# Second attention: the next group's weight tiles transposed by VectorE in 32x32 blocks instead of by TensorE

## The chip, the cores and the metric

The kernel runs on one core of a Trainium2 chip. The metric is the device time of one execution in microseconds (us), given as the median of several runs. A profiled execution has a time of its own and, inside it, a span: the stretch from the first to the last instruction that the profiler recorded.

## The reference

A transformer block on `x` (8 x 128 x 512, float32). First comes a low-rank stage with a small attention over the eight rows, then the attention that this case is about, then a feed-forward part with low-rank experts. The second attention, cut to what matters:

```python
q = jnp.einsum('bsd,ed->bse', x, Wq).reshape(bsz, seqlen, HQ, D)   # 32 query heads of 128
k = jnp.einsum('bsd,ed->bse', x, Wk).reshape(bsz, seqlen, HK, D)   # 8 key/value heads
v = jnp.einsum('bsd,ed->bse', x, Wv).reshape(bsz, seqlen, HK, D)
q, k = _rope(_rmsnorm(q, q_norm_w), pos), _rope(_rmsnorm(k, k_norm_w), pos)
kc, vc = k_cache[block_table], v_cache[block_table]                # 512 cached keys per row
scores = einsum(q, concat(kc, k)) * SCALE                          # masked where not valid
probs = jax.nn.softmax(scores, axis=-1)
o = jnp.einsum('bhqk,bkhd->bqhd', probs, concat(vc, v))
return jnp.einsum('bse,de->bsd', o.reshape(bsz, seqlen, HQ * D), Wo)
```

## The kernel before

TensorE multiplies in fp32r, a rounded float32. To keep precision every operand X is split into a high part X_hi (X rounded to fp32r) and a low part X_lo = X - X_hi, and every product is three matmuls (`mm3`, lines 739 to 741). So each operand has to be transposed, rounded and subtracted before it is used.

The second attention is a loop over 8 groups g (one key/value head with its 4 query heads) and, inside it, 8 steps n (one row of the batch): 64 steps. A step of the instruction streams holds, for batch row n: the scores of 4 heads (`ps_a`, `ps_b`), the values product of the step before (`ps_o<-pT,v`), the projection of the next row's q (`ps_q`) and k, v (`project_kv`, into `ps_o` from `wa`), and the output projection of the step before (`out_proj`, from `wo`). Everything is written out by hand, engine by engine, and joined by semaphores; each engine works through its own list in order.

Transposes on TensorE go through a ring of two PSUM banks, `ps_t`. A group of four 128x128 transposes (`transposed`, line 948) fills a bank. ScalarE copies it out rounded (`copy_hi`, line 1366), VectorE subtracts (`copy_lo`, line 1788), and the bank after next waits for that subtraction (`t_lo`). Each step has the ring groups K (cached keys), D0 to D3 (the probabilities of the four heads), q, and DS (the probabilities of the step's own keys).

While group g is worked on, the ten weight tiles of group g+1 (four of Wq, one each of Wk and Wv, four of Wo; 128x512 each) are brought in. `W_COUNT` puts one of them into steps n = 0, 2, 4, 6, two into n = 1, 3, 5, and none into n = 7, in groups 0 to 6: 70 tiles in all. The group of step n = 7 already projects with them. A tile is loaded by SyncE into one of two slots of `wtile` (line 486), transposed as a ring group W between the scores of heads 0 and 1 and the values product, copied by ScalarE into `wa_hi` or `wo_hi` and subtracted by VectorE into `wa_lo` or `wo_lo`. SyncE loads the tile after next into the slot when TensorE is through with it.

The other names that the prediction uses, in the order of one step:

- `least(h)` on VectorE (line 1912) reads head h's scores, adds the mask and finds the extreme, `mn`. ScalarE's `exponentials(h)` (line 1443) follows. `normalise(0)` and `normalise(1)` are on VectorE (lines 1919, 1924), `normalise(2)` and `normalise(3)` on ScalarE (line 1453). D0 to D3 transpose the results.
- `output_hi` and `output_lo` (lines 1413, 1867) split the values product. `own_v_hi` (line 1449) rounds the row's own v.
- `copy_kv` (line 1370) takes the projected k and v out of `ps_o`, and TensorE's `out_proj` waits for it (`kv_copied`). `square_k` (line 1376) sums the squares of k.
- GpSimd does, in a step: four gathers of cached keys (line 622), the high and low parts of v (lines 687, 689, 692), three gathers of cached values, `stats_k` (lines 653, 656: the norm of k, which waits for `square_k`), the fourth gather of values, and `stats_q` (lines 661 to 666: the norm of q). VectorE's `rope_k` (line 1821) waits for `stats_k`. TensorE's `project_kv` waits for the own v's low part (`vs_lo`, line 692). `least(0)` of the next step waits for `stats_q` (`st_done`).
- After `rope_k`, VectorE makes `qT_lo`. The last ring group DS waits for it and ends TensorE's step.

Of the kernel before, what the change touches and what calls it, by code (L numbers as in the profile page):

```python
# [17 lines left out]
F32 = mybir.dt.float32  # L18
# [37 lines left out]
def block_program(nc, x, ids_adapter, table_pages, cache_len, lora_a, lora_b, w_qkv, w_proj, wq, wk, wv, wo,  # L56
# [4 lines left out]
    with ctx:  # L61
# [69 lines left out]
        wa_lo = at("wa_lo", [P, 2, NC_, PW], F32R, 160)  # L131
        wtile = at("wtile", [P, 2, HID], F32, 184)
# [133 lines left out]
        wt_in = [sem(f"wt_in{i}") for i in range(2)]  # L266
        tab_in = [sem(f"tab_in{i}") for i in range(2)]
# [72 lines left out]
        def groups_of(n, last):  # L340
            if last:
                w = [f"L{i}" for i in range(7) if i // 2 + 1 == n] + [f"Y{i}" for i in range(2) if N - 2 + i == n]
            else:
                w = [f"W{W_FIRST[n] + i}" for i in range(W_COUNT[n])] if W_COUNT[n] else []
            nxt = not (last and n == N - 1)
            return w + ["K"] * nxt + ["D0", "D1", "D2"] + ["q"] * nxt + ["D3", "DS"]

# [64 lines left out]
        def hi_lo_target(name, g, kpar1, lo):  # L412
# [13 lines left out]
            return w_dst((wa_hi, wa_lo)[lo], (wo_hi, wo_lo)[lo], (g + 1) % 2, int(name[1:])), HID  # L426
# [20 lines left out]
        def _(sp):  # L447
# [28 lines left out]
            def load_wtile(g, t, slot):  # L476
# [9 lines left out]
                sp.dma_start(wtile[:, slot, :], src).then_inc(wt_in[slot], 16)  # L486
# [37 lines left out]
            def step(g, n, last):  # L524
# [6 lines left out]
                for name in groups_of(n, last):  # L531
                    if name[0] == "W" and int(name[1:]) + 2 < TILES_W:
                        t = int(name[1:])
                        wait_alone(sp, t_full, base + t_index(n, name, last)[0] + 1)
                        load_wtile(g + 1, t + 2, t % 2)
                    elif name[0] == "W" and g + 2 < G:
                        t = int(name[1:])
                        wait_alone(sp, t_full, base + t_index(n, name, last)[0] + 1)
# [39 lines left out]
        def _(pool):  # L578
# [92 lines left out]
            def step(g, n, last):  # L671
# [29 lines left out]
                if not (last and n == N - 1):  # L701
                    stats_q(J + 1, 1 - par)
                if n == N - 1 and not last:
# [40 lines left out]
        def _(pe):  # L744
# [206 lines left out]
            def w_tile(idx, bank, t, arrivals):  # L951
                pe.wait_ge(wt_in[t % 2], arrivals)
                transposed(idx, bank, [(c, wtile[:, t % 2, c * P:(c + 1) * P]) for c in range(NC_)])

# [108 lines left out]
            def step(g, n, first, last):  # L1063
# [39 lines left out]
                for name in names:  # L1103
# [6 lines left out]
                    if name[0] == "W":  # L1110
                        t = int(name[1:])
                        w_tile(*idx(name), t, g * (16 * TILES_W // 2) + 16 * (t // 2 + 1))
# [5 lines left out]
                if nxt:  # L1118
# [3 lines left out]
                    if n == N - 1:  # L1122
                        pe.wait_ge(t_lo, base + t_index(6, "W9", last)[0] + 1 + 2)
# [290 lines left out]

# [674 lines left out]
```

## Time and profile before

| | |
|---|---|
| time, median of 3 runs | 1568.53 us (1563.63 to 1569.09) |
| profiled execution | 1554.2 us, span 1552.5 us |
| busy share of the span | TensorE 97%, VectorE 76%, ScalarE 58%, GpSimd 57% |
| mean granted TensorE clock | 0.991 |
| transposes of `wtile` on TensorE | 280 (70 tiles of four) |

The second attention is the stretch from about 332 us to 1500 us of the span. The profiled execution is some 14 us shorter than the median. In each timeline below a row gives start, duration, engine, line, operation, what is written from what is read, and, in brackets, how long the engine was idle before it and what ended that. An engine starts its next instruction a little before the shown end of the one before, so two starts give the real pace.

### The profile page before, as it was taken

The numbers are of one execution on the slowest core, as the hardware profiler recorded it, in microseconds if no ns is written. First come the engines' busy times: TensorE is split into PE (matmuls) and PEld (weight loads), VectorE is DVE, ScalarE is ACT, GpSimd is POOL, SyncE is SP. The second block draws the span as 40 slices with busy tenths as digits, with TensorE's granted clock in tenths as the row PEclk, the third lists the DMA queues.
The fourth block names the chain that finished last, engine by engine and source line by source line (L and its number), as shares of the span: only waits on it lengthen the run. The fifth ranks groups of instructions, "written<-read, shape, count | busy, mean of one in ns | idle before, by whom it ended". The sixth has DMA issues, their size and how long they took to land.

```text
span 1552.5 us, 27376 instructions
## 1 busy us (share of the span) xinstructions
PE 1509.9 (97%) x8984; PEld 1293.2 (83%) x8984; DVE 1180.2 (76%) x2668; ACT 893.2 (58%) x2308; POOL 879.2 (57%) x1231
## 2 busy tenths in 40 slices
PE   6899999989999999999999999999999999999997
PEld 4788888778888888888888888888888888888885
DVE  3666665767888888888888878888887888777865
ACT  2433333356666666666666666666666666666641
POOL 1111234236667666766676676667666766676521
PEclk8999999999999999999999999999999999999999
DMA  6654555322222222222222222222222222311102
GB/s 209 209 161 134 148 165 162 77 82 70 69 71 73 69 71 61 76 70 70 64 72 71 71 66 70 70 71 72 70 72 66 70 69 65 89 59 48 42 27 82
DMA packets 74085, 133.39 MB, mean 86 GB/s; under 512 B 17426, under 2 KB 27026, under 8 KB 73946
## 3 DMA queue, kind: packets, MB, share of 16 engines
q1 hardware_dynamic: 56482, 97.56, 21.2%
q0 software_dynamic: 16464, 33.85, 7.5%
q8 instruction: 74, 1.21, 0.3%
q14 instruction: 65, 0.53, 0.1%
q10 hardware_dynamic: 1000, 0.23, 0.1%
HBM read 107.47 MB, written 7.34 MB: 74 GB/s over the span
## 4 chain that ended last, share of the span: by engine, by line
PE 91%; DVE 3%; ACT 2%; issue 2%; POOL 1%; DMA 1%; ACTq 0%; POOLq 0%; DVEq 0%; SPq 0%
PE ps_t L948 15%; PE ps_o L739 11%; PE ps_o L741 10%; PE ps_o L740 10%; PE ps_b L739 5%; PE ps_b L741 5%; PE ps_b L740 5%; PE ps_q L741 4%; PE ps_q L740 4%; PE ps_q L739 4%; PE ps_t L762 3%; PE ps_a L739 3%; PE ps_a L793 3%; PE ps_a L741 3%; PE ps_a L740 3%
## 5 line engine op out<-in xcount | busy, mean ns | idle before, releaser
L1443 ACT ACTIVATE sm<-sm,mn 128x640 f32<-128x640 f32 x256 | 211.4, 826 | 234.5 <-DVE mn L1912 234.5
L1788 DVE TENSOR_TENSOR pT_lo<-ps_t,pT_hi 128x512 fp32r<-128x512 f32 x320 | 220.2, 688 | 113.5 <-ACT pT_hi L1366 113.3
L622 POOL DMA_INDIRECT kraw<-in_L_cond_k_cache_dram,idx_a x200 | 197.5, 988 | 89.1 <-issue 74.3
L1366 ACT ACTIVATE pT_hi<-ps_t 128x512 fp32r<-128x512 f32 x320 | 188.5, 589 | 84.7 <-PE ps_t L948 84.7
L622 POOL DMA_INDIRECT vraw<-in_L_cond_v_cache_dram,idx_a x200 | 198.7, 994 | 59.6 <-issue 59.3
L948 PE MATMUL ps_t<-ident,sm 128*128 128x128 f32 x1280 | 195.7, 275 | 3.2 <-ACT sm L1453 1.5
L948 PEld LDWEIGHTS ps_t<-ident,sm 128*128 128x128 f32 x1280 | 147.9, 140 | 51.4 <-DVE qT_lo L1788 17.9
L639 POOL TENSOR_TENSOR z<-pairs_p,zl 128x128 f32<-128x128 f32 x160 | 57.9, 402 | 206.8 <-DVE pairs_p L1652 206.8
L739 PE MATMUL ps_o<-pT_lo,v_hi 128*128 128x512 f32 x320 | 129.8, 406 | 0.0
L741 PE MATMUL ps_o<-pT_hi,v_hi 128*128 128x512 f32 x320 | 125.5, 392 | 0.0
L740 PE MATMUL ps_o<-pT_hi,v_lo 128*128 128x512 f32 x320 | 124.9, 390 | 0.0
L1912 DVE CUSTOM_DVE_ANT_0 sm<-ps_a,mask,qs 128x640 f32<-128x640 f32 x128 | 112.6, 879 | 11.2 <-PE ps_a L741 4.6
L739 PE MATMUL ps_o<-wo_lo,oT_hi 128*128 128x512 f32 x256 | 117.6, 460 | 2.3
L1912 DVE CUSTOM_DVE_ANT_0 sm<-ps_b,mask,qs 128x640 f32<-128x640 f32 x128 | 112.9, 882 | 3.8 <-issue 0.4
L739 PE MATMUL ps_q<-wa_lo,x2T_hi 128*128 128x512 f32 x256 | 105.8, 413 | 0.0
L1453 ACT ACTIVATE sm<-sm,rd 128x640 f32<-128x640 f32 x128 | 105.6, 825 | 0.0
L741 PE MATMUL ps_q<-wa_hi,x2T_hi 128*128 128x512 f32 x256 | 101.5, 396 | 0.0
L741 PE MATMUL ps_o<-wo_hi,oT_hi 128*128 128x512 f32 x256 | 101.4, 396 | 0.0
L740 PE MATMUL ps_o<-wo_hi,oT_lo 128*128 128x512 f32 x256 | 100.6, 393 | 0.0
L740 PE MATMUL ps_q<-wa_hi,x2T_lo 128*128 128x512 f32 x256 | 100.6, 393 | 0.0
L739 PE MATMUL ps_a<-kT_lo,qT_hi 128*128 128x320 f32 x256 | 90.3, 353 | 1.7 <-DVEq L1861 1.7
L689 POOL TENSOR_TENSOR v_lo<-vraw,v_hi 128x512 fp32r<-128x512 f32 x64 | 82.6, 1291 | 11.9 <-POOL v_hi L687 11.5
(257 smaller groups left out, 4370.1 us busy)
## 6 DMA issues: line engine op xcount, KB each, us to landing
fv<-st SPq DMA_DIRECT2D x128, 128.0 KB, 2.3
tab<-tab_scratch SPq DMA_DIRECT2D x64, 256.0 KB
wraw<-n_L_attn_weight_qkv_dram SPq DMA_DIRECT2D x8, 1536.0 KB, 7.3
wpraw<-_L_attn_weight_proj_dram SPq DMA_DIRECT2D x8, 1024.0 KB, 9.4
mask<-mask_scratch SPq DMA_DIRECT2D x64, 128.0 KB
wtile<-in_L_cond_Wq_dram SPq DMA_DIRECT2D x28, 256.0 KB
wtile<-in_L_cond_Wo_dram SPq DMA_DIRECT2D x28, 256.0 KB
kraw<-in_L_cond_k_cache_dram,idx_a POOLq DMA_INDIRECT x200, 2.6
```

The source lines that it names most:

```text
L622: pool.indirect_dma_start(raw[:, par, c, :], None, rows_d, bass.IndirectOffsetOnAxis(idx[:, k:k + 1].bitcast(U32), 0)).then_inc(arrived[pa ...
L639: ins = pool.tensor_tensor(out, pr, zz, ALU.mult)
L689: pool.tensor_tensor(v_lo[:, 0:KC, :], vraw[:, par, :, :], v_hi[:, 0:KC, :].bitcast(F32), ALU.subtract).then_inc(vc_lo, 1)
L739: pe.matmul(o, l_hi, r_lo, start=start, stop=False)
L740: pe.matmul(o, l_lo, r_hi, start=False, stop=False)
L741: return pe.matmul(o, l_hi, r_hi, start=False, stop=stop)
L948: mm = pe.transpose(ps_t[bank][:, o * P:(o + 1) * P], i, ident[:])
L1366: act.activation(dst, src, ACT.Copy).then_inc(t_hi, 1)
L1443: act.activation(sm[:, h, :], sm[:, h, :], ACT.Exp, bias=mn[:, h:h + 1], scale=-1.0, accum_out=den[:, h:h + 1]).then_inc(e_done, 1)
L1453: act.activation(sm[:, h, :], sm[:, h, :], ACT.Copy, scale=rd[:, h:h + 1]).then_inc(p_act, 1)
L1788: dve.tensor_tensor(lo, src, hi.bitcast(F32), ALU.subtract).then_inc(t_lo, 1)
L1912: dve.tensor_tensor_reduce(out=sm[:, h, :].rearrange("p (b k) -> p b k", b=2), in0=halves, in1=mask[:, par, :].rearrange("p (b k) -> p b k ...
```

## The change

- SyncE loads a tile in four DMAs, one for each fourth of the partitions, so that piece (c, i) of 32 inputs of every weight row (128 bytes) lands in partitions 32i to 32i+31. Partition 32i+p holds weight rows 4p to 4p+3.
- VectorE turns the whole tile with one instruction that transposes 32x32 blocks (`turn`), into `wa_turn` or `wo_turn`. These lie where `wa_lo` and `wo_lo` lie. Neighbouring elements of a transposed row are written four float32, 16 bytes, apart.
- ScalarE makes the high part from that (`turned_hi`), at the same place of its list as before.
- GpSimd makes the low part in place at the end of its step, after `stats_q` and ahead of the next step's gathers.
- TensorE's ring group W is gone. The steps of group 7 and its late weights keep theirs.

```diff
+        wa_turn = at("wa_turn", [P, 2, NC_, PW], F32, 160)
+        wo_turn = at("wo_turn", [P, 2, HG, HID], F32, 64)
...
-                sp.dma_start(wtile[:, slot, :], src).then_inc(wt_in[slot], 16)
+                blocks = src.rearrange("e (c i a) -> i e c a", c=NC_, i=4)
+                for i in range(4):
+                    sp.dma_start(wtile[32 * i:32 * i + 32, slot, :], blocks[i]).then_inc(wt_in[slot], 16)
...
+                for t in tiles_of(n, last):
+                    wait_alone(pool, wt_hi, g * TILES_W + t + 1)
+                    pool.tensor_tensor(w_dst(wa_lo, wo_lo, (g + 1) % 2, t), w_dst(wa_turn, wo_turn, (g + 1) % 2, t),
+                                       w_dst(wa_hi, wo_hi, (g + 1) % 2, t).bitcast(F32),
+                                       ALU.subtract).then_inc(wt_lo, 1)
...
-                    if name[0] == "W":
-                        t = int(name[1:])
-                        w_tile(*idx(name), t, g * (16 * TILES_W // 2) + 16 * (t // 2 + 1))
...
-                        pe.wait_ge(t_lo, base + t_index(6, "W9", last)[0] + 1 + 2)
+                        pe.wait_ge(wt_lo, (g + 1) * TILES_W)
...
                 exponentials(0)
                 if w:
                     group(w[0])
+                if tiles:
+                    turned_hi(g, tiles[0])
                 exponentials(1)
                 if len(w) > 1:
                     group(w[1])
+                if len(tiles) > 1:
+                    turned_hi(g, tiles[1])
                 if not first:
                     output_hi(J)
...
+                def turn(t):
+
+                    dve.wait_ge(wt_in[t % 2], (g * (TILES_W // 2) + t // 2 + 1) * 64)
+                    dve.transpose(w_dst(wa_turn, wo_turn, (g + 1) % 2, t).rearrange("p c (b j) -> p j c b", j=4),
+                                  wtile[:, t % 2, :].rearrange("p (j c a) -> p j c a", j=4, c=NC_)
+                                  ).then_inc(wt_turned, 1)
...
                 least(1)
                 if w:
                     group(w[0])
+                if tiles:
+                    turn(tiles[0])
                 normalise(0)
                 normalise(1)
                 if len(w) > 1:
                     group(w[1])
+                if len(tiles) > 1:
+                    turn(tiles[1])
                 if not (first and n < 1):
                     output_lo(J)
```

Two places where this moves instructions. The first is VectorE in a step with two tiles, before:

```order
L1788 TENSOR_TENSOR wa_lo<-ps_t,wa_hi 128x4x128 [waits t_hi]
L1919 RECIPROCAL rd<-den 128x1 [waits e_done]
L1924 TENSOR_SCALAR sm<-sm,rd 128x640 [waits r_done]
L1919 RECIPROCAL rd<-den 128x1 [waits e_done]
L1924 TENSOR_SCALAR sm<-sm,rd 128x640 [waits r_done]
L1788 TENSOR_TENSOR wa_lo<-ps_t,wa_hi 128x4x128 [waits t_hi]
L1867 TENSOR_TENSOR oT_lo<-ps_o,oT_hi 128x512 [waits o_hi]
```

The same place after the change, again VectorE's list in a step with two tiles:

```order
L1911 STREAM_TRANSPOSE wa_turn<-wtile 128x4x4x32 [waits wt_in1]
L1944 RECIPROCAL rd<-den 128x1 [waits e_done]
L1949 TENSOR_SCALAR sm<-sm,rd 128x640 [waits r_done]
L1944 RECIPROCAL rd<-den 128x1 [waits e_done]
L1949 TENSOR_SCALAR sm<-sm,rd 128x640 [waits r_done]
L1911 STREAM_TRANSPOSE wa_turn<-wtile 128x4x4x32 [waits wt_in0]
L1884 TENSOR_TENSOR oT_lo<-ps_o,oT_hi 128x512 [waits o_hi]
```

The subtraction of the tile stood behind ScalarE's rounding; now the transpose stands ahead of it, in the same two positions, and waits for the load. Line numbers differ because the changed file is longer.

The second place is GpSimd's list from `stats_q` of a step with two tiles to the own v's low part of the next step, after the change:

```order
L669 TENSOR_SCALAR ms<-ss 128x4 [waits sqq_done]
L672 TENSOR_TENSOR rs<-ms,halfs 128x4 [waits st_pool]
L674 TENSOR_SCALAR qs<-rs 128x4 [waits st_pool]
L713 TENSOR_TENSOR wa_lo<-wa_turn,wa_hi 128x4x128 [waits wt_hi] x2
L630 DMA kraw<-in_L_cond_k_cache_dram,idx_a 128x128 [waits t_full]
L630 DMA kraw<-in_L_cond_k_cache_dram,idx_a 128x128 x3
L695 CAST v_hi<-vraw 128x512 [waits vg_in0,pv_full]
L697 TENSOR_TENSOR v_lo<-vraw,v_hi 128x512 [waits vc_hi]
L700 TENSOR_TENSOR v_lo<-kvown,v_hi 128x128 [waits vs_hi]
```

The row `wa_lo<-wa_turn,wa_hi` is new on this engine; the rows around it stood next to each other before.

## Rows read from the trace of the kernel before

**Rows 1.** TensorE's timeline: starts of five steps (L739 `ps_a`), three places between

```profile
805.72 0.39 PE L739 MATMUL ps_a<-kT_lo,qT_hi 128*128 128x320 f32 x1
...
817.29 0.28 PE L739 MATMUL ps_o<-wa_lo,x2T_hi 128*128 128x256 f32 x1
...
823.74 0.39 PE L739 MATMUL ps_a<-kT_lo,qT_hi 128*128 128x320 f32 x1
...
837.18 0.60 PE L948 MATMUL ps_t<-ident,sm 128*128 128x128 f32 x4
837.82 0.50 PE L739 MATMUL ps_o<-wo_lo,oT_hi 128*128 128x512 f32 x1
...
842.18 0.39 PE L739 MATMUL ps_a<-kT_lo,qT_hi 128*128 128x320 f32 x1
...
896.67 0.39 PE L739 MATMUL ps_a<-kT_lo,qT_hi 128*128 128x320 f32 x1
...
914.24 0.39 PE L739 MATMUL ps_a<-kT_lo,qT_hi 128*128 128x320 f32 x1
```

**Rows 2.** GpSimd's timeline: one cycle in full places, then the change of group

```profile
820.61 0.19 POOL L653 TENSOR_SCALAR ms<-ss 128x1 f32<-128x1 f32 x1 [1.80 <-ACT rope_b L1376]
...
824.83 0.23 POOL L666 TENSOR_SCALAR qs<-rs 128x4 f32<-128x4 f32 x1 [0.20 <-POOL rs L664]
...
831.24 1.29 POOL L689 TENSOR_TENSOR v_lo<-vraw,v_hi 128x512 fp32r<-128x512 f32 x1 [0.19 <-POOL v_hi L687]
832.49 0.46 POOL L692 TENSOR_TENSOR v_lo<-kvown,v_hi 128x128 fp32r<-128x128 f32 x1
...
839.06 0.19 POOL L653 TENSOR_SCALAR ms<-ss 128x1 f32<-128x1 f32 x1 [2.25 <-ACT rope_b L1376]
...
911.11 0.19 POOL L653 TENSOR_SCALAR ms<-ss 128x1 f32<-128x1 f32 x1 [1.06 <-ACT rope_b L1376]
...
929.15 0.19 POOL L653 TENSOR_SCALAR ms<-ss 128x1 f32<-128x1 f32 x1
```

**Rows 3.** VectorE's timeline: `rope_k` of one step, then a step with two tiles

```profile
821.59 0.35 DVE L1821 SCALAR_TENSOR_TENSOR rope_a<-kvown,rs,tab 128x128 f32<-128x128 f32 x1
...
826.52 0.88 DVE L1912 CUSTOM_DVE_ANT_0 sm<-ps_b,mask,qs 128x640 f32<-128x640 f32 x1
...
828.07 0.69 DVE L1788 TENSOR_TENSOR wa_lo<-ps_t,wa_hi 128x512 fp32r<-128x512 f32 x1 [0.67 <-ACT wa_hi L1366]
...
829.59 0.55 DVE L1924 TENSOR_SCALAR sm<-sm,rd 128x640 f32<-128x640 f32 x1
...
833.59 0.88 DVE L1912 CUSTOM_DVE_ANT_0 sm<-ps_a,mask,qs 128x640 f32<-128x640 f32 x1
```

**Rows 4.** ScalarE's timeline in the same step with two tiles

```profile
827.94 0.82 ACT L1443 ACTIVATE sm<-sm,mn 128x640 f32<-128x640 f32 x1
...
830.08 0.60 ACT L1413 ACTIVATE oT_hi<-ps_o 128x512 fp32r<-128x512 f32 x1 [0.75 <-PE ps_o L741]
...
832.35 0.60 ACT L1366 ACTIVATE pT_hi<-ps_t 128x512 fp32r<-128x512 f32 x1 [0.98 <-PE ps_t L948]
...
834.50 0.83 ACT L1443 ACTIVATE sm<-sm,mn 128x640 f32<-128x640 f32 x1 [1.56 <-DVE mn L1912]
...
837.38 0.38 ACT L1370 ACTIVATE kvown<-ps_o 128x256 f32<-128x256 f32 x1 [0.50 <-PE ps_o L741]
```

**Rows 5.** Groups by line and shape, 512 elements each: busy us, mean ns

```profile
L1557 DVE TENSOR_SCALAR turns<-turns 128x512 f32<-128x512 f32 x2 | 0.9, 428 | 0.1
L1562 DVE SCALAR_TENSOR_TENSOR sin_t<-turns,turns 128x512 f32<-128x512 f32 x1 | 0.7, 693 | 0.0
L1423 ACT ACTIVATE wbT_hi<-ps_t 128x512 fp32r<-128x512 f32 x4 | 2.3, 579 | 0.0
L1423 ACT ACTIVATE ebT<-ps_t 128x512 f32<-128x512 f32 x1 | 1.1, 1057 | 0.0
```

**Rows 6.** DMA queues from 1349 to 1360 us: packets, MB, share of 16 engines

```profile
q1 hardware_dynamic: 1550, 1.00, 30.2%
```

More of the change, by code:

```diff
@@ L266, in block_program @@
         wt_in = [sem(f"wt_in{i}") for i in range(2)]
+        wt_turned = sem("wt_turned")
+        wt_hi = sem("wt_hi")
+        wt_lo = sem("wt_lo")
         tab_in = [sem(f"tab_in{i}") for i in range(2)]
@@ L340, in groups_of, with tiles_of @@
         def groups_of(n, last):
+            w = []
             if last:
                 w = [f"L{i}" for i in range(7) if i // 2 + 1 == n] + [f"Y{i}" for i in range(2) if N - 2 + i == n]
-            else:
-                w = [f"W{W_FIRST[n] + i}" for i in range(W_COUNT[n])] if W_COUNT[n] else []
             nxt = not (last and n == N - 1)
             return w + ["K"] * nxt + ["D0", "D1", "D2"] + ["q"] * nxt + ["D3", "DS"]
+        def tiles_of(n, last):
+            return [W_FIRST[n] + i for i in range(W_COUNT[n])] if W_COUNT[n] and not last else []
         PER_G = sum(len(groups_of(n, False)) for n in range(N))
@@ L530, in step @@
                     load_wtile(g + 1, 1, 1)
-                for name in groups_of(n, last):
-                    if name[0] == "W" and int(name[1:]) + 2 < TILES_W:
-                        t = int(name[1:])
-                        wait_alone(sp, t_full, base + t_index(n, name, last)[0] + 1)
+                for t in tiles_of(n, last):
+                    if t + 2 < TILES_W:
+                        wait_alone(sp, wt_turned, g * TILES_W + t + 1)
                         load_wtile(g + 1, t + 2, t % 2)
-                    elif name[0] == "W" and g + 2 < G:
-                        t = int(name[1:])
-                        wait_alone(sp, t_full, base + t_index(n, name, last)[0] + 1)
+                    elif g + 2 < G:
+                        wait_alone(sp, wt_turned, g * TILES_W + t + 1)
                         load_wtile(g + 2, t + 2 - TILES_W, t % 2)
@@ L702, in step @@
                     stats_q(J + 1, 1 - par)
+                for t in tiles_of(n, last):
+                    wait_alone(pool, wt_hi, g * TILES_W + t + 1)
+                    pool.tensor_tensor(w_dst(wa_lo, wo_lo, (g + 1) % 2, t), w_dst(wa_turn, wo_turn, (g + 1) % 2, t),
+                                       w_dst(wa_hi, wo_hi, (g + 1) % 2, t).bitcast(F32),
+                                       ALU.subtract).then_inc(wt_lo, 1)
                 if n == N - 1 and not last:
@@ L1413, in output_hi, with turned_hi @@
                 act.activation(oT_hi[:, :, :].rearrange("p h m -> p (h m)"), ps_o[:, :], ACT.Copy).then_inc(o_hi, 1)
+            def turned_hi(g, t):
+                act.wait_ge(wt_turned, g * TILES_W + t + 1)
+                act.activation(w_dst(wa_hi, wo_hi, (g + 1) % 2, t),
+                               w_dst(wa_turn, wo_turn, (g + 1) % 2, t), ACT.Copy).then_inc(wt_hi, 1)
             def late_copy(idx, bank, i):
@@ L1453, in normalise @@
                     act.activation(sm[:, h, :], sm[:, h, :], ACT.Copy, scale=rd[:, h:h + 1]).then_inc(p_act, 1)
-                w = [m for m in names if m[0] in "WLY"]
+                w = [m for m in names if m[0] in "LY"]
+                tiles = tiles_of(n, last)
                 exponentials(0)
@@ L1887, in step @@
                 nxt = not (last and n == N - 1)
-                w = [m for m in names if m[0] in "WLY"]
+                w = [m for m in names if m[0] in "LY"]
+                tiles = tiles_of(n, last)
+                def turn(t):
[3 more added lines that the diff above has]
+                                  ).then_inc(wt_turned, 1)
                 def group(name):
```

6 lines of the change are left out of this document (1 added, 5 removed).

## The prediction

> **What bounds the kernel now.** I read the page's busy shares first: TensorE is busy 97% of the span. Then TensorE's timeline, for the length of a step [rows 1]. The step from 805.72 to 823.74 has one weight tile and takes 18.02 us, the next has two and takes 18.44, and the one from 896.67 to 914.24 has none and takes 17.57. So a tile costs TensorE 0.44 us, although its four transposes alone last 0.35, and a group of 8 steps takes 4 x 18.02 + 3 x 18.45 + 17.57 = 145.0 us. Next come the engines beside it, for how much air each has, since the change hands them work. GpSimd's cycle is best counted from one `stats_k` to the next, because it stands idle only there: from 820.61 to 839.06, with 2.25 us idle at the end, and 1.80 or 1.06 in other steps [rows 2]. Its own work in a cycle is 18.45 - 2.25, so 16.20 us, and about 16.27 with the hand-over. At the change of group it has extra index work: 911.11 to 929.15 is 18.04 us, without any idle time [rows 2]. VectorE and ScalarE have more air in sum, but at fixed places: ScalarE is idle 0.98 us before D0's high part [rows 4].
>
> **TensorE's share.** 70 tiles x 0.44 us = 30.8 us come off its list. That is the whole possible gain, and it comes only as far as no other engine holds TensorE.
>
> **GpSimd's share.** The subtraction has the form of `v_lo`, 128x512 from two SBUF operands, at 1.25 us from start to start (831.24 to 832.49) [rows 2]. Its wait (`wt_hi`) is long met by the end of a step, so nothing comes on top. The cycle is then 16.27 + 1.25 = 17.52 us after a step with one tile and 16.27 + 2.50 = 18.77 after one with two. A TensorE step without tiles takes 17.57. So after n = 1, 3, 5 GpSimd reaches the next `stats_k` late. Who waits for that: `rope_k` starts at 821.59, while `stats_k` began at 820.61 and needs 0.95, so nothing lies between them [rows 2, 3]. Behind `rope_k` VectorE makes `qT_lo`, and DS, the last group of TensorE's step, waits for it. No cover is left, so lateness goes straight into the step. Queued behind the subtractions on GpSimd are also the key gathers and the own v's low part, for which `project_kv` waits. From `stats_k` to the end of that low part are 12.34 us now, 14.84 with two subtractions. TensorE wants it 11.57 us into the step (817.29 - 805.72) [rows 1], less 0.44. It comes 0.6 late, but this is a part of the same lateness and is not counted twice.
>
> **VectorE's and ScalarE's share.** Call the transpose's time d. In a one-tile step it delays exp(1) by under 1.2 us, and the idle time before D0's high part plus the earlier end of the values product takes that up as long as d stays under about 1.4. Such a step gains its 0.44 us. In a two-tile step it does not fit. `turned_hi` now waits for `turn`, which can't start before `least(1)` is through (826.52 + 0.81) [rows 3]. From there: 827.33 + d + 0.53 is the start of exp(1), against 827.94 [rows 4]. VectorE's normalise(1) stands 1.65 behind the start of exp(1) and is left 0.47 later. Then comes the second `turn`, again d, and ScalarE stands still for it. Its rounding (0.5) is followed by the high parts of the output, of v and of K (0.5 + 0.2 + 0.5), and only then D0's. With d = 1.17 the places are 829.03 for exp(1), 831.82 for the end of the second `turn`, and 833.54 for D0's high part instead of 832.35. Three VectorE subtractions in a row (output, K, D0) add a little, so `least(2)` starts at 834.88 instead of 833.59 [rows 3], and exp(2) at 835.79 instead of 834.50 [rows 4]. D2 can't start before about 838.1. TensorE would be there at 837.18 - 0.88 = 836.30 [rows 1]. `copy_kv` is behind the same ScalarE work and ends at 838.56 instead of 837.76, and `out_proj` follows it: 0.80 us later than the 837.82 of now. So a two-tile step takes 19.25 us instead of 18.45. Each 0.1 us of d moves this by 0.2 us.
>
> **How long is d?** No row shows this instruction. The nearest from below is a one-input VectorE instruction on 512 elements in its fast form, 0.43 us; a three-operand one takes 0.69 [rows 5]. But the output is scattered 16 bytes apart. The one instruction before that writes so is ScalarE's `ebT`: 1.057 us against 0.579 for the same 512 elements written densely [rows 5], so 0.48 us more. I take 0.69 + 0.48 = 1.17 us, since this is the only row of a computing engine that writes with that stride. 0.69 is the other serious value. The ends are 0.43 and 1.65 (the scatter's cost twice over).
>
> The Trainium skill (Advanced Engine Details and Errata, Memory Cachelines) says that SBUF works in lines of 16 bytes and that accesses which each go to a new line pay. By that rule the row of `ebT` carries over to VectorE and d is near 1.2. Against it, the skill's VectorE page (VectorE: DVE Perf Modes, The three transpose paths) gives 311 ns for a 128x128 bf16 transpose, and its page Vector Engine (DVE) Microarchitecture Reference (The reshape front-end and per-opcode configuration) says that the transposer sustains one element per cycle and lane. An estimate from these pages is about 0.7 us, so the sum would be that of the dense rival below. No row here decides between them.
>
> **DMA.** A tile becomes 2048 pieces, 128 for each of the 16 engines. In a stretch with many small packets (the loads of `ebraw`, 256 bytes a piece) 1550 packets took 30.2% of 16 x 11 us, 34 ns each [rows 6]. That gives about 4 us a tile, and each slot is free a whole step (over 17 us) ahead. SyncE's issues are four for one, and the tables behind them are needed a step later. I cost it at nothing; if a tile did land late, VectorE's list would stop at `turn`.
>
> **The sum.** Taken from `stats_k` to `stats_k`. Into a two-tile step (three in a group): 18.45 before, and 17.57 - 14.45 + 16.12 = 19.24 after (`stats_k` begins 820.61 - 805.72 - 0.44 = 14.45 into a one-tile step and 839.06 - 823.74 + 0.80 = 16.12 into a two-tile step) [rows 1, 2], so +0.79. Out of a two-tile step (three): 18.01 before; GpSimd's 18.77 after, so +0.76. From n = 6 to 7: 17.57 either way. From n = 7 to 0: GpSimd's 18.04 either way, so the 0.44 us of step 0 are lost. A group gains 3 x 1.55 = 4.65 us in length, and seven groups 32.6 us. The profiled execution would go from 1554.2 to about 1587. The same on the median: 1568.5 + 32.6 = 1601.
>
> **The rivals.**
> 1. Dense rate: d = 0.69. The interval into a two-tile step becomes 18.45 - 0.17, and GpSimd's +0.76 stays: 3 x 0.59 x 7 = 12.4 us, 1581. For it: every VectorE row of 512 float32 that isn't in the fast form takes about this long. Against it: none of them scatters. The two pages named last above speak for this rival.
> 2. Fast: d = 0.43. The interval into a two-tile step loses another 0.52, and 3 x 0.07 x 7 = 1.5 us remain: 1570, no change that can be measured.
> 3. Faster than before: TensorE decides. If GpSimd's lateness did not reach DS (because the norm or the gathers finish sooner when nothing is waited for) and the ScalarE chain had room, every interval would be 17.57: per group 3 x 0.88 + 3 x 0.44 = 3.96 us less, 27.7 in all: 1541. It decides once GpSimd's cycle after two tiles is under 17.57 instead of 18.77. Against it: GpSimd's cycles add up to 4 x 17.52 + 3 x 18.77 + 18.04 = 144.4 us a group with no idle time at all, against 145.0 now.
> 4. Dearer transposes: d = 1.65 gives 2 x 0.48 x 21 = 20 us more: 1621, and from about 1.4 on one-tile steps begin to lose too.
> 5. Late pieces: the loads of 128 bytes take over a step. It would take four times the packet price above, and adds some us per group: 1610 or more.
>
> **How the numbers follow.** Forecast 0.50, rival 1 0.25, rival 2 0.07, rival 3 0.07, rival 4 0.07, rival 5 0.04. The range of 1569 to 1618 holds the forecast, the dense and the fast rival and most of the late pieces, and leaves out the dearer and the all-gain case. A measurement of this kernel can tell 0.5% (8 us) from no change. Rival 3 is faster, 0.07. Rival 2 with a small tail of rival 1 is within it, 0.11. The rest is slower, 0.82.
>
> **What would show it.** Mean time of the transpose: 1.1 to 1.25 us for the forecast. Steps on TensorE: two-tile steps near 19.25, the steps behind them near 18.8 (17.57 + 1.20), n = 7 near 17.6, the last group unchanged. `stats_k` with no idle time before it behind two-tile steps. TensorE's idle time ended by `qT_lo` or `v_lo` in even steps and by ScalarE's `sm` or `kvown` in odd ones. It would be wrong if GpSimd still stood idle before every `stats_k`, or if `turn` waited for DMA.

## The result and the profile after

In the comparison made for the change, the two kernels ran beside each other on one chip:

| | before | after |
|---|---|---|
| median | 1568.8 us (1563.6 to 1569.1) | 1590.3 us (1586.6 to 1590.7) |
| ratio | | 1.014 (95% interval 1.011 to 1.017) |
| profiled execution, span | 1554.2, 1552.5 us | 1589.9, 1588.1 us |

(A fourth execution of the kernel before took 2129 us. It is left out of the range but counted in the median; without it the median is 1568.5 us and the difference below 21.8 us.)

The change makes the kernel 21.5 us slower. Between the two profiles it is 35.7 us. The forecast of 32.6 us lies between these, and why there are two answers is a part of the finding.

The page of the changed kernel: the span, the busy lines, the DMA counts and the chain that ended last.

```profile
span 1588.1 us, 27096 instructions
...
PE 1498.4 (94%) x8704; PEld 1259.3 (79%) x8704; DVE 1200.9 (76%) x2668; ACT 896.5 (56%) x2308; POOL 974.9 (61%) x1301
...
DMA packets 211846, 133.39 MB, mean 84 GB/s; under 512 B 164146, under 2 KB 173746, under 8 KB 211706
...
q1 hardware_dynamic: 194242, 97.57, 24.0%
...
PE 47%; POOL 17%; issue 14%; DVE 13%; ACT 7%; DMA 1%; ACTq 0%; POOLq 0%; DVEq 0%
```

TensorE lost 280 matmuls and 11.5 us of work (1509.9 before), and its share fell from 97% to 94%: it waits more than it was relieved of. Only 47% of the chain is TensorE's, and 17% is GpSimd's. The same line of the kernel before:

```profile
PE 91%; DVE 3%; ACT 2%; issue 2%; POOL 1%; DMA 1%; ACTq 0%; POOLq 0%; DVEq 0%; SPq 0%
```

TensorE's timeline, group 3, the rows that answer to [rows 1]: the start of a step with two tiles (842.43), of the step behind it (862.07), the next (880.65), and of n = 7 (918.76) with the group's end.

```profile
842.43 0.39 PE L752 MATMUL ps_a<-kT_lo,qT_hi 128*128 128x320 f32 x1
...
862.07 0.39 PE L752 MATMUL ps_a<-kT_lo,qT_hi 128*128 128x320 f32 x1
...
873.72 0.35 PE L752 MATMUL ps_o<-wa_lo,x2T_hi 128*128 128x256 f32 x1 [0.36 <-POOL v_lo L700]
...
880.24 0.66 PE L961 MATMUL ps_t<-ident,sm 128*128 128x128 f32 x4 [0.21 <-DVE qT_lo L1805]
880.65 0.39 PE L752 MATMUL ps_a<-kT_lo,qT_hi 128*128 128x320 f32 x1
...
918.76 0.39 PE L752 MATMUL ps_a<-kT_lo,qT_hi 128*128 128x320 f32 x1
...
936.35 0.39 PE L752 MATMUL ps_a<-kT_lo,qT_hi 128*128 128x320 f32 x1
```

The two-tile step takes 19.64 us (18.44 before), the step behind it 18.58 (18.02), and n = 7 takes 17.59 (17.57). In the step behind, TensorE waits for `v_lo` and, at DS, for `qT_lo`, the two places that hang on GpSimd.

GpSimd's timeline in the same two steps, answering to [rows 2]: `stats_k`, the two subtractions, the next `stats_k`.

```profile
858.94 0.19 POOL L661 TENSOR_SCALAR ms<-ss 128x1 f32<-128x1 f32 x1 [2.73 <-ACT rope_b L1382]
...
863.48 2.55 POOL L713 TENSOR_TENSOR wa_lo<-wa_turn,wa_hi 128x512 fp32r<-128x512 f32 x2
...
877.52 0.19 POOL L661 TENSOR_SCALAR ms<-ss 128x1 f32<-128x1 f32 x1
```

Ahead of 858.94, in the two-tile step, it is idle for 2.73 us. Behind the two subtractions the idle time is gone: 18.58 us of work from one `stats_k` to the next, and TensorE's step has the same 18.58.

ScalarE, VectorE and TensorE in the two-tile step from 842.43, answering to [rows 3, 4]:

```profile
846.01 1.08 DVE L1911 STREAM_TRANSPOSE wa_turn<-wtile 128x512 f32<-128x512 f32 x1
...
849.33 1.11 DVE L1911 STREAM_TRANSPOSE wa_turn<-wtile 128x512 f32<-128x512 f32 x1
```

```profile
847.12 0.64 ACT L1424 ACTIVATE wa_hi<-wa_turn 128x512 fp32r<-128x512 f32 x1 [0.88 <-DVE wa_turn L1911]
...
850.48 0.63 ACT L1424 ACTIVATE wa_hi<-wa_turn 128x512 fp32r<-128x512 f32 x1 [1.91 <-issue]
...
854.44 0.83 ACT L1455 ACTIVATE sm<-sm,mn 128x640 f32<-128x640 f32 x1 [1.67 <-DVE mn L1937]
...
857.26 0.38 ACT L1376 ACTIVATE kvown<-ps_o 128x256 f32<-128x256 f32 x1 [0.45 <-PE ps_o L754]
```

```profile
855.81 0.28 PE L754 MATMUL ps_o<-wa_hi,x2T_hi 128*128 128x256 f32 x1
856.62 0.66 PE L961 MATMUL ps_t<-ident,sm 128*128 128x128 f32 x4 [0.52 <-issue]
857.70 0.50 PE L752 MATMUL ps_o<-wo_lo,oT_hi 128*128 128x512 f32 x1 [0.43 <-ACT kvown L1376]
```

ScalarE stands 0.88 and 1.91 us ahead of the two roundings, and each starts at the end of its transpose (the second at 850.48, the transpose ends at 850.44). Everything behind is late by what the prediction worked out: exp(2) 12.01 us into the step (forecast 12.05), D2 at 14.19 (14.36). Only the last two rows don't fit it. ScalarE is free at 856.81 and TensorE's last projection matmul began at 855.81, and yet the copy of k and v starts at 857.26. This row is taken up below.

### The profile page after: what moved, and what is told of

Its sections match the earlier page's. It is cut to its first block, busy times and chain, and to the rows that moved or that the text cites. A ratio compares the mean times of both kernels' runs of the same rounds, so it can differ in the third digit from the quotient of the medians.

```text
span 1588.1 us, 27096 instructions
## 1 busy us (share of the span) xinstructions
PE 1498.4 (94%) x8704; PEld 1259.3 (79%) x8704; DVE 1200.9 (76%) x2668; ACT 896.5 (56%) x2308; POOL 974.9 (61%) x1301
## 4 chain that ended last, share of the span: by engine, by line
PE 47%; POOL 17%; issue 14%; DVE 13%; ACT 7%; DMA 1%; ACTq 0%; POOLq 0%; DVEq 0%
POOL kraw L630 6%; PE ps_o L754 6%; PE ps_o L752 5%; POOL vraw L630 5%; PE ps_o L753 5%; PE ps_t L961 5%; PE ps_b L752 3%; PE ps_b L754 3%; PE ps_b L753 3%; PE ps_t L775 3%; PE ps_a L806 3%; POOL v_lo L697 2%; ACT sm L1455 2%; DVE pT_lo L1805 2%; DVE sm L1937 2%
## 5 line engine op out<-in xcount | busy, mean ns | idle before, releaser
L752 PE MATMUL ps_o<-pT_lo,v_hi 128*128 128x512 f32 x320 | 125.7, 393 | 0.0
L1944 DVE RECIPROCAL rd<-den 128x1 f32<-128x1 f32 x256 | 40.9, 160 | 77.2 <-ACT sm L1455 60.4
```

The costliest lines, as they stand in the source:

```text
L752: pe.matmul(o, l_hi, r_lo, start=start, stop=False)
```

## The experiments

They ran in four sets, each on one chip with the kernel before beside it. The kernel before lay at 1568.55 us in the first set (experiments 1 to 4), and at 1554.79 (5 and the first two of 6), 1554.58 (the last of 6, and 7) and 1554.49 us (the last of 7) in the other three. I call these the upper and the lower level. The mean granted TensorE clock of the kernel before is 0.99 at both, so the clock does not tell them apart. "Group" below is the mean length of groups 1 to 6, from TensorE's step starts.

**1. The loads alone.**

```diff
-                sp.dma_start(wtile[:, slot, :], src).then_inc(wt_in[slot], 16)
+                blocks = src.rearrange("e (c i a) -> i e c a", c=NC_, i=4)
+                for i in range(4):
+                    sp.dma_start(wtile[32 * i:32 * i + 32, slot, :], blocks[i]).then_inc(wt_in[slot], 16)
```

> The kernel before, with only the loads changed: each of the 70 weight tiles comes in four DMAs of 128-byte pieces, as in the changed kernel. TensorE still transposes it, so the weights of groups 1 to 7 stand in another order than they should. Theory (the loads cost nothing): the time of the kernel before, 1568.5 us within 3 us, steps 17.57 / 18.0 / 18.45 as before. Rival (the pieces cost something: late tiles, or gathers slowed by four times as many packets): 5 us or more above, with TensorE's W transposes or the GpSimd gathers starting later. Since the changed kernel lies 21.5 us above the kernel before, this run says how much of that is DMA.

Measured: 1569.28 us, ratio 1.0004 (0.9995 to 1.0013). Its 137,762 packets more than before (211,847 against 74,085) cost nothing that can be measured. DMA is out as a cause. In the profile of this run 28 signals come late; what that means and how it is counted stands with the prediction's number below.

**2. Without GpSimd's subtractions.**

```diff
-                    wait_alone(pool, wt_hi, g * TILES_W + t + 1)
-                    pool.tensor_tensor(w_dst(wa_lo, wo_lo, (g + 1) % 2, t), w_dst(wa_turn, wo_turn, (g + 1) % 2, t),
-                                       w_dst(wa_hi, wo_hi, (g + 1) % 2, t).bitcast(F32),
-                                       ALU.subtract).then_inc(wt_lo, 1)
+                    pass
```

> The changed kernel without GpSimd's subtractions: no low parts of the 70 tiles are made, and TensorE reads the high parts in their place, the same number of matmuls of the same shape. Theory (two causes, each in its own steps): the steps behind a two-tile step fall from 18.58 to 17.57 us, the two-tile steps keep about 19.5, since there ScalarE waits for the transposes; 3 x 1.0 us a group, 21 us in all: 1569 us. Rival A (GpSimd is the whole cause, the two-tile steps are long because GpSimd's lateness reaches into them): all steps go to 17.6, 1545 us or less. Rival B (ScalarE is the whole cause): nothing moves, 1590 us.

Measured: 1573.3 us, ratio 1.0026 (1.0016 to 1.0037). Most steps behind a two-tile step take 17.57 us (two of 18 in groups 1 to 6 take 18.2), most two-tile steps still 19.5 to 20.0 and a few 19.0 to 19.1. So both causes are real and each sits in its own steps: rival A and rival B fall. The time is 4 us above the expected one, since two-tile steps grew by 0.2 us.

**3. The transpose writes side by side.**

```diff
-                    dve.transpose(w_dst(wa_turn, wo_turn, (g + 1) % 2, t).rearrange("p c (b j) -> p j c b", j=4),
+                    dve.transpose(w_dst(wa_turn, wo_turn, (g + 1) % 2, t).rearrange("p c (j b) -> p j c b", j=4),
```

> The changed kernel with one thing altered: the transpose writes its 512 elements side by side instead of 16 bytes apart, so the weight columns come in another order. Theory (the scatter is what makes the transpose take 1.08 us): the instruction takes 0.69 us, the two-tile steps shorten by 2 x 0.39 us, 21 x 0.78 = 16 us in all: 1574 us, the steps behind them stay at 18.6 because GpSimd still holds them. Rival (the transposer itself takes 1.08 us for 512 float32, whatever the output's stride): nothing moves, 1590 us.

Measured: 1569.2 us, ratio 1.0003 (0.9993 to 1.0012). VectorE's groups by shape (busy us, mean ns), the changed kernel first, then this run:

```profile
L1911 DVE STREAM_TRANSPOSE wa_turn<-wtile 128x512 f32<-128x512 f32 x42 | 45.7, 1088 | 0.0
```

```profile
L1911 DVE STREAM_TRANSPOSE wa_turn<-wtile 128x512 f32<-128x512 f32 x42 | 29.5, 703 | 0.0
```

The scatter costs 0.385 us of 1.088. The last number of the rows says that neither waited for a load. Two-tile steps fell to 18.29 us, and most of those behind lie at 18.83 (18.6 to 18.8 before). The two-tile steps fell by more than 0.77 us, and so the time is 5 us below the expected one. The rest is the late copy, which is gone from them.

**4. The rounding one step later.**

```diff
+                if n and not last:
+                    for t in tiles_of(n - 1, last):
+                        turned_hi(g, t)
                 exponentials(0)
                 if w:
                     group(w[0])
-                if tiles:
-                    turned_hi(g, tiles[0])
                 exponentials(1)
                 if len(w) > 1:
                     group(w[1])
-                if len(tiles) > 1:
-                    turned_hi(g, tiles[1])
```

> The changed kernel with ScalarE's rounding of a step's tiles moved to the head of its next step, ahead of exp(0), where ScalarE stands idle for 2.0 us. ScalarE then never waits for a transpose. GpSimd's subtractions keep their place. Theory (ScalarE's wait makes the two-tile steps long, GpSimd the steps behind them): the two-tile steps fall from 19.5 to about 17.6, the steps behind them go to GpSimd's full cycle of 18.77, a group from 149.8 to 4 x 17.57 + 3 x 18.77 + 18.04 = 144.6, the whole to 1590 - 7 x 5.2 = 1554 us. Rival (VectorE's own two transposes make the two-tile step long, by what they push back in VectorE's list, not through ScalarE): those steps stay above 19 us, and the time above 1580.

Measured: 1559.3 us, ratio 0.994 (0.993 to 0.996). This moves only where ScalarE rounds, and at the upper level it turns a kernel that is 1.4% slower into one that is 0.6% faster. TensorE's step starts in group 2: n = 4 (behind a step with two tiles), n = 5 (with two), n = 6.

```profile
695.91 0.39 PE L752 MATMUL ps_a<-kT_lo,qT_hi 128*128 128x320 f32 x1
...
714.76 0.39 PE L752 MATMUL ps_a<-kT_lo,qT_hi 128*128 128x320 f32 x1
...
732.39 0.39 PE L752 MATMUL ps_a<-kT_lo,qT_hi 128*128 128x320 f32 x1
```

The two-tile step (714.76 to 732.39) takes 17.63 us, with both transposes still in VectorE's list; so it was ScalarE's wait, not VectorE's load, that made it 19.5. The step behind a two-tile step goes to 18.85 us (695.91 to 714.76), GpSimd's full cycle. The run is 5 us above the expected 1554: some of these steps take 19.0, and a few two-tile steps 18.8.

Being faster than the kernel before holds for the upper level only. An undisturbed group of this run is 17.92 + 3 x 17.62 + 3 x 18.87 + 17.63 = 145.0 us, the same as the 145.0 of the kernel before, and the mean group of its profile is 145.7. What it wins there fits its 2 late signals, where the run with pieces only has 28. It was not timed at the lower level, where the rows let one expect no gain over the kernel before.

**5. The kernel before again, and one signal moved.** The first profile of the kernel before was 14 us shorter than its median. A second one:

> The kernel before, unchanged, for a second profile. The first profiled execution took 1554.2 us, 14 us less than the median of the timed ones. In the traces of the changed kernel and of the run with pieces only, TensorE's signal that k and v are projected (which ScalarE's copy of them waits for) often comes 0.3 to 0.7 us later than 0.30 us after the start of the last matmul, up to the end of the D2 transposes behind it; in the first profile of the kernel before it never does. Theory: that is the 14 us, and this profile takes about 1568 us and has 20 to 30 such late signals. Rival (the profiler's own doing, or another cause): it takes 1554 again, or 1568 with none of them late.

Measured: 1554.2 us, no signal late by more than 0.17 us, and the kernel before timed beside it at 1554.8. The theory's 1568 us did not come, and the rival's number did, but not by the profiler's doing, since profiled and timed executions agree here. The kernel before has two levels, and its first profile was of the lower one. What a late signal costs:

```diff
-                mm.then_inc(akv_full, 1)
...
+                    for c in range(KC):
+                        mm = pe.transpose(ps_t[bank][:, c * P:(c + 1) * P], sm[:, h, c * P:(c + 1) * P], ident[:])
+                        if held and c == 2:
+                            mm.then_inc(akv_full, 1)
```

> The kernel before with one signal moved: TensorE signals the projected k and v not with the last matmul of that product but with the third of the four D2 transposes that follow it, so ScalarE's copy always starts about 0.85 us after that matmul's start instead of 0.32. Theory (the late signal costs what it is late, since ScalarE's copy and with it the output projection stand on the path): every step is 0.53 us longer than an undisturbed one, 18.1 / 18.5 / 19.0 us, 63 x 0.53 = 33 us on top of the 1554.2 us of the first profile: 1587 us. Rival (the copy has room, the late signals only go along with longer steps): no more than 3 us over the kernel before, 1568 to 1572 us.

Measured: 1581.9 us, ratio 1.0174 (1.0160 to 1.0188), 27 us above the kernel before. The copy started 0.65 us after the last matmul in steps with two tiles and 0.95 in most with one, and these steps became 18.78 and 18.65 us, 0.33 and 0.63 longer. That is one for one (0.65 - 0.32 and 0.95 - 0.32). So the copy of k and v has no room at all; only the size was off, since I had expected 0.85 in all of them. Why the third transpose's signal comes at two different times isn't known.

**6. The work placed elsewhere.** The changed kernel with the edit of experiment 4, with `W_COUNT` 1, 2, 2, 2, 1, 2, 0, 0 and the low parts shared out:

```diff
-                for t in tiles_of(n, last):
+                for t in (tiles_of(n - 1, last)[:1] if n else []):
                     wait_alone(pool, wt_hi, g * TILES_W + t + 1)
...
                 reciprocal(3)
+                for t in (tiles_of(n - 1, last)[1:] if n else []):
+                    dve.wait_ge(wt_hi, g * TILES_W + t + 1)
+                    dve.tensor_tensor(w_dst(wa_lo, wo_lo, (g + 1) % 2, t), w_dst(wa_turn, wo_turn, (g + 1) % 2, t),
+                                      w_dst(wa_hi, wo_hi, (g + 1) % 2, t).bitcast(F32),
+                                      ALU.subtract).then_inc(wt_lo2, 1)
```

> The changed kernel with its work placed elsewhere: ScalarE rounds a step's tiles at the head of its next step; two tiles fall into n = 1, 2, 3, 5, one into n = 0 and 4, none into 6 and 7; GpSimd makes the low part of the first tile of the step before, never more than one a step, and VectorE that of the second, behind its reciprocal for head 3, where it stands idle. Loads and transpose are those of the changed kernel. Theory (GpSimd's cycle with one subtraction is 17.52 us, under TensorE's 17.57, and nothing waits for a transpose): all steps 17.6 us but the one at the change of group, 18.04; a group 141.3 instead of 149.8 us, 1590 - 7 x 8.5 = 1530 us, and few late signals, as in the run with the roundings late (3 of 63). Rival (VectorE has no room for 2 x 1.08 and 0.69 us in one step and becomes the bound): two-tile steps of 18.2 us and more, 4 a group, 1547 us or more.

Measured: 1542.8 us, ratio 0.993 (0.992 to 0.994). This version computes the reference and beats both kernels, and unlike experiment 4 it does so at the lower level. Group 143.8 instead of the expected 141.3: the steps n = 1, 3 and 5 with two tiles take 18.0 to 18.5 us on average, n = 2 with two takes 17.7 in most groups, those with none 17.6 and 17.7, and 8 signals are late, by 6.1 us in sum. Neither theory's number is met; it lies between them.

> The run with the work placed elsewhere, and the transpose writing side by side. For that a tile is loaded in 16 DMAs instead of 4 (the same 2048 pieces of 128 bytes), so that partition 32i + p holds weight rows p, 32 + p, 64 + p and 96 + p and the columns come out in order. The transpose takes 0.70 us instead of 1.09. Theory (no transpose is on the path once nothing waits for it): the same time as that run within 3 us, about 1530 us. Rival A (VectorE is still what bounds the two-tile steps): 0.77 us less in each of 28 steps, 20 us faster than that run. Rival B (SyncE's 16 issues, some 10 us a tile, hold up the tables and masks behind them on its queue): slower than that run by 5 us or more.

```diff
-                blocks = src.rearrange("e (c i a) -> i e c a", c=NC_, i=4)
+                blocks = src.rearrange("(j p) (c i a) -> i j p c a", j=4, c=NC_, i=4)
                 for i in range(4):
-                    sp.dma_start(wtile[32 * i:32 * i + 32, slot, :], blocks[i]).then_inc(wt_in[slot], 16)
+                    for j in range(4):
+                        sp.dma_start(wtile[32 * i:32 * i + 32, slot, j * P:(j + 1) * P],
+                                     blocks[i, j]).then_inc(wt_in[slot], 16)
```

Measured: 1584.0 us, ratio 1.019 (1.018 to 1.021), 41 us slower than the run above. Rival B, and dearer than thought. SyncE's queue (start, time of the issues, what is loaded) and the transpose that waits for it, in the step from 823.65 to 843.74:

```profile
820.93 10.20 SPq L498 DMA_DIRECT2D wtile<-in_L_cond_Wk_dram  x16
831.24 0.52 SPq L482 DMA_DIRECT2D tab<-tab_scratch  x1
```

```profile
832.73 0.71 DVE L1914 STREAM_TRANSPOSE wa_turn<-wtile 128x512 f32<-128x512 f32 x1 [3.49 <-DMA wtile<-in_L_cond_Wk_dram]
```

Sixteen issues take SyncE 10.2 us, 0.64 each. Two tiles a step are over 20 us of issuing in steps of 17.6, the queue falls behind, and VectorE stands 3.49 us for a tile. It is the number of DMAs that costs here, not the number of packets: these are 225,293, only 6% more than in the changed kernel. SyncE's queue has 16% of the chain that ended last, against 0% in the run above. Some 6 of the 41 us are of another kind: 14 signals are late, by 12.0 us in sum, against 6.1.

> The run with the work placed elsewhere, with one thing altered: the transpose writes side by side, so the weight columns come in another order (the loads stay four DMAs a tile). The transpose takes 0.70 us. Theory (in the placed-elsewhere run the two-tile steps are 18.0 to 18.4 us because VectorE's two transposes delay the low part of the cached keys and with it D0 and D1): 2 x 0.38 us less on VectorE brings these steps to 17.6 to 17.8, 4 x 0.35 x 7 = 10 us under the 1542.8 us of that run at the lower level of before, 0.980 to 0.985 of the kernel before. Rival (late signals alone make them long): the same 0.993 as that run.

The edit is the one line of experiment 3 on top of the placed-elsewhere run. Measured: 1528.7 us, ratio 0.984 (0.983 to 0.986), as the theory said. Most two-tile steps take 17.57 to 17.73, a group 142.1 on average, and no signal is late. Of the 14 us between this run and the one with the scatter, 6.1 are that run's late signals. The two ran in different sets, so whether these vanish with the scatter or with the chip isn't shown. The other 8 go with VectorE's scatter. This is where the change could go if the columns came in order for nothing; no run here has that.

**7. The changed kernel at the lower level.**

> The kernel before, unchanged, once more. So far its executions lie at two levels: 1568.5 us where it was timed beside the changed kernel and in the first set of experiments, 1554.8 us in the second set; both profiles are of the lower level, without one late signal of the projected k and v. Theory (the 14 us are late signals, and they go with the chip or the set): if this set lies at 1568, the profile has 20 or more of them and steps of 18.7 us; if it lies at 1554, it has none. Rival: a profile at 1568 without late signals, its 14 us elsewhere.

> The changed kernel, unchanged, beside the kernel before in a set of its own. In its first profile 23 of 63 signals were late. Theory (in its two-tile steps TensorE stands still before D2, and the signal is late there on any chip; only the other steps depend on the chip): at the upper level of before (1568) it takes 1590 us again, ratio 1.014; at the lower level (1554) it keeps its late signals and takes 1587 to 1590, ratio 1.021 to 1.023, so that the change costs 33 us, as forecast. Rival (the late signals come and go with the chip for both): 1576 us at the lower level, ratio 1.014.

Measured: the kernel before 1555.5 us, with one signal late, by 0.13 us, and 1554.6 timed. The changed kernel 1582.8 us, ratio 1.019 (1.017 to 1.021): 28.2 us slower at this level. That lies between the theory's 1587 to 1590 and the rival's 1576, so neither number was met, and the theory's reason was wrong: no signal is late here. In the same places (group 3, n = 1) the copy starts when ScalarE is free, with no idle time in front:

```profile
813.41 0.28 PE L754 MATMUL ps_o<-wa_hi,x2T_hi 128*128 128x256 f32 x1
814.22 0.66 PE L961 MATMUL ps_t<-ident,sm 128*128 128x128 f32 x4 [0.53 <-ACT sm L1465]
814.76 0.50 PE L752 MATMUL ps_o<-wo_lo,oT_hi 128*128 128x512 f32 x1
```

```profile
814.32 0.38 ACT L1376 ACTIVATE kvown<-ps_o 128x256 f32<-128x256 f32 x1
```

The two-tile steps are 19.0 to 19.1 us here, those behind 18.85, a group 149.3. The kernel before ran once more, for a profile at the upper level:

> The kernel before, unchanged, once more, for a profile at the upper level. So far it was timed at 1568.5 us in two sets and at 1554.7 in two others, and all three profiles of it are of the lower level, with no late signal. Theory: if this set lies at 1568, the profile has 20 to 30 late signals of the projected k and v, as the run with pieces only had (28) at that level. Rival: 1568 without late signals. If the set lies at 1554 again, it tells nothing new.

It took 1556.1 us, at the lower level again, with three signals late by 0.21 us at most, so it tells nothing new.

## Why the prediction was right, and where its number was not

**Slower, by its two causes.** Both hold. Experiment 2 takes GpSimd's term away and leaves ScalarE's; experiments 3 and 4 take ScalarE's and leave GpSimd's. Without late signals (experiment 7) the interval into a two-tile step is 19.08 us (forecast 19.24) and out of it 18.84 (18.77); n = 6 to 7 17.58 (17.57), n = 7 to 0 17.88 (18.04). A group grew by 4.2 us (forecast 4.65) and the whole by 28.2 (32.6).

**d.** Forecast 1.17 us, measured 1.088. By the prediction's own slope, 0.2 us a step for each 0.1 of d, that takes 0.16 from 19.24 and gives the 19.08 measured. The decomposition 0.69 + 0.48 is right in kind: 0.703 dense and 0.385 for the scatter. The 0.48 came from ScalarE's row `ebT`; on VectorE the same stride costs 0.1 us less. The Trainium skill (Advanced Engine Details and Errata, Memory Cachelines) says that accesses which each touch another 16-byte line pay. The 0.385 us agree with it, but no run here tries another stride, so that the line is the reason isn't shown. The Trainium skill (Vector Engine (DVE) Microarchitecture Reference, The reshape front-end and per-opcode configuration) says that the transposer sustains one element per cycle and lane. The prediction's estimate of about 0.7 us from it is met with a dense output only: 0.703 us, close to the 0.693 of the 512-element VectorE row that isn't in the fast form [rows 5].

**The dense rival** named 18.45 - 0.17 = 18.28 us for the two-tile step; experiment 3 measured 18.29. It priced the steps right, and its condition was false. Its total, 12.4 us more than before, is met only against undisturbed steps: the mean group is 146.8 us against 145.05, 7 x 1.74 = 12.2 us. At the upper level, where experiment 3 was timed, it costs nothing (1.0003), which fits its 5 late signals, where the run with pieces only has 28.

**The third rival**, faster, asks for two things: that "the ScalarE chain had room", and that "GpSimd's cycle after two tiles is under 17.57 instead of 18.77". Experiment 4 gives ScalarE room and leaves GpSimd its full cycle: the kernel gains on the changed one (1559.3 against 1590.3), but an undisturbed group is only as long as before. Experiment 6 sets up both conditions, and the kernel is faster than before (1542.8 against 1554.8). So the rival named its conditions rightly, and the changed kernel meets neither.

**DMA at nothing** was right (1.0004), and so was the warning about SyncE's issues in it: four a tile are free, sixteen cost 41 us.

**The number.** 1601 us was forecast and 1590.3 measured. The step that failed is the last of the sum: "The same on the median: 1568.5 + 32.6". The profile's own number, "from 1554.2 to about 1587", is 3 us from the profiled 1589.9, but that is luck: this execution is of the upper level, and the profiled one of the lower level took 1583.3. The front of the document says that the profiled execution is 14 us shorter than the median, and the prediction carried the difference over without asking where these 14 us are. As far as the traces show, most of them sit in one place which the change also touches:

TensorE signals the projected k and v with its last matmul. In the first profile of the kernel before, ScalarE's copy starts 0.32 us after that matmul's start, in every step. In the run with pieces only it is often later, although both engines do the same work at the same times. Two steps with one tile of experiment 1, the same to 0.01 us up to that point. The undisturbed one:

```profile
677.43 0.28 PE L743 MATMUL ps_o<-wa_hi,x2T_hi 128*128 128x256 f32 x1
...
678.19 0.50 PE L741 MATMUL ps_o<-wo_lo,oT_hi 128*128 128x512 f32 x1
```

```profile
677.75 0.38 ACT L1372 ACTIVATE kvown<-ps_o 128x256 f32<-128x256 f32 x1 [0.50 <-issue]
```

The late one:

```profile
823.10 0.28 PE L743 MATMUL ps_o<-wa_hi,x2T_hi 128*128 128x256 f32 x1
823.22 0.60 PE L950 MATMUL ps_t<-ident,sm 128*128 128x128 f32 x4
824.55 0.50 PE L741 MATMUL ps_o<-wo_lo,oT_hi 128*128 128x512 f32 x1 [0.73 <-ACT kvown L1372]
```

```profile
824.11 0.38 ACT L1372 ACTIVATE kvown<-ps_o 128x256 f32<-128x256 f32 x1 [1.19 <-PE ps_o L743]
```

The copy starts 1.01 us after the matmul instead of 0.32, TensorE's output projection waits 0.73 us, and the step is 18.71 instead of 18.02 us. The trace's record of semaphores has the signal itself 0.99 us after the matmul's start. In the first profile of the kernel before it is at 0.30 in all steps. The next signal, that of the D2 transposes, is late too: at 1.05 us, against 0.73 there. In the undisturbed step shown above D2's signal is also late, at 1.00, while the copy went in time. So signals of TensorE come late one by one or together. D2's has room: in the second profile of the kernel before it is late in more than 20 steps, and the time is that of the first profile. The one for k and v has none (experiment 5). TensorE's matmuls start in time up to there; whether they also end in time isn't shown, since the trace's ends of matmuls are modelled.

I counted for each profile how long ScalarE stood ready for the copy beyond the usual 0.32 us (the 23 and 3 of the expectations were counted less strictly):

| profile | level | late | sum | span |
|---|---|---|---|---|
| before, first | lower | 0 | 0 us | 1552.5 us |
| pieces only | upper | 28 | 11.9 us | 1564.5 us |
| changed kernel, first | upper | 18 | 6.6 us | 1588.1 us |
| changed kernel, again | lower | 0 | 0 us | 1581.5 us |

Of the other profiles at the upper level, experiment 2 has 20 late signals (7.4 us), experiment 3 has 5 (2.4) and experiment 4 has 2 (0.8). At the lower level the three later profiles of the kernel before have at most 3 (0.6 us), but the run with the work placed elsewhere has 8 (6.1) and the one with 16 DMAs a tile 14 (12.0). So late signals go with the level for these two kernels, and not for every schedule.

Where no signal is late, the steps of the run with pieces only are those of the kernel before (18.02 and 18.46 us). In groups 1 to 6 it is 10.0 us longer than the kernel before, and 9.6 us of late signals lie there. That the whole spans differ by 12.0 us, and all its late signals sum to 11.9, is partly chance: 2.5 us of the 12.0 lie ahead of the second attention. For the changed kernel the equality of 1588.1 - 1581.5 = 6.6 us with its 6.6 is chance as well. In groups 1 to 6 its execution at the upper level is 3.1 us longer, with 4.9 us of late signals: the two-tile steps are 6.2 us longer and the steps behind them 3.0 shorter, and why these are shorter isn't known.

By the medians the upper level costs the kernel before about 14 us and the changed kernel 7.5 (1590.3 - 1582.8). A reason that fits: in the steps behind a two-tile step, where the run with pieces only loses 0.69 us to each late signal, TensorE now waits for GpSimd ahead of that product, and no signal is late. That this wait is what keeps the signals in time is argued and not shown. So the change costs 28.2 us at one level and 21.5 at the other. The 1590.3 is thus the undisturbed 1554.6 + 28.2 plus 7.5, and the forecast of 1601 was 1554.2 + 32.6 plus 14.3. Of the 10.7 us between them, 4.4 are the size of the terms, and 6.8 are the upper level's cost, taken from a kernel that has no room there for one that has some (less 0.4 between the two bases).

That the kernel before itself has its late signals at the upper level is shown by none of its own profiles, since all four are of the lower level; it rests on the run with pieces only, which has the same time (1.0004).

## What to carry to other kernels

An engine with much idle time in sum may still have none where its work is wanted. Moving 0.6 us of rounding per tile into ScalarE's 2 us gap one step later was worth 31 us here (1590.3 to 1559.3), and the engine that was to be relieved, TensorE, decided neither the two-tile steps nor those behind them. Place a new producer and its consumer in different steps of the software pipeline, and cost each engine's cycle in the heaviest step, not in the mean one. And where the profiled execution and the median differ by more than the effect sought, find out where they differ before a difference from the one is added to the other.

## What the runs showed of the hardware

- A signal of TensorE came 0.30 us after its matmul's start in all steps of the first profile of the kernel before, but up to 1.01 us after it in the run with pieces only, 1.43 in the changed kernel and 1.63 with the work placed elsewhere. How often goes with the chip or the time (four sets: 1568.5, 1554.8, 1554.6, 1554.5 us for one kernel, each within 6 us) and with the kernel: with the roundings late it happened twice at the upper level, with the work placed elsewhere 8 times at the lower one. What holds it isn't known.
- VectorE's 32x32 transpose of 128x512 float32: 0.703 us written densely, 1.088 us with neighbouring elements 16 bytes apart.
- 137,762 packets more over the kernel cost nothing measurable (1.0004), while each DMA costs SyncE's queue 0.64 us to issue (16 in 10.2 us).
